# Second cross attention: the weights' products moved into the block of the turns, and another order of squares and queries

## What is computed

```
rmsnorm(x, w) = x * rsqrt(mean(x*x) + 1e-6) * w
slots = layernorm(x)                     # 16 x 64 x 256
inputs = rmsnorm(ctx, input_norm_w)      # its keys Wk and values Wv
three times:
    q     = rmsnorm(slots, slot_norm_w) @ Wq
    att   = softmax over the slots of (keys @ q * D**-0.5), normed over the keys
    u     = att summed with the values
    slots = gru_cell(u, slots, wih, whh, bih, bhh)
x = x + slots
```

## Time and profile before

| | us |
|---|---|
| three runs: median | 3616.66 |
| three runs: lowest and highest | 3610.97, 3619.45 |
| profiled execution, own time | 3608.83 |
| its span, first to last instruction | 3607.0 |
| from the start of the s1_pre block to its end, about | 1289.5 to 1299.3 |
| block of the turns, about | 1299.3 to 1798.2 |

### The profile page before, as it was taken

How to read it: one execution, slowest core, us unless ns; L and a number is a source line. 1 busy time by engine, 2 the same in 40 slices (tenths; PEclk the granted TensorE clock), 3 DMA queues, 4 the chain that set the end, 5 groups by cost and what they waited for, 6 DMA issues and landing times. The chain is left out here.

```text
span 3607.0 us, 91217 instructions
## 1 busy us (share of the span) xinstructions
PE 3381.5 (94%) x39608; PEld 2382.1 (66%) x39608; DVE 2091.1 (58%) x4136; ACT 1719.2 (48%) x3158; POOL 817.4 (23%) x464
## 2 busy tenths in 40 slices
PE   7999999979998979999989998999999789999996
PEld 4777777656676658888854455777777565665554
DVE  5666666754444257777654484556656456555337
ACT  4777777623332168887645452444444342112124
POOL 2776777410110000000031121011010003331002
PEclk9999999999999999999998999999999889999998
DMA  2111111030101415354010002112110002320530
GB/s 78 45 39 39 39 50 46 6 99 29 38 1 50 161 48 177 111 174 166 2 42 24 0 0 70 41 41 60 41 59 23 25 15 93 109 99 12 178 126 17
DMA packets 154953, 223.35 MB, mean 62 GB/s; under 512 B 39327, under 2 KB 134235, under 8 KB 154428
## 3 DMA queue, kind: packets, MB, share of 16 engines
q1 hardware_dynamic: 154556, 217.51, 18.2%
HBM read 216.44 MB, written 1.05 MB: 60 GB/s over the span
## 5 line engine op out<-in xcount | busy, mean ns | idle before, releaser
L3361 POOL TENSOR_TENSOR x_sc<-x_sc,h_T 128x2048 f32<-128x2048 f32 (+1 forms) x105 | 443.6, 4269 | 199.1 <-ACT h_T L3588 199.1
L3171 ACT ACTIVATE x_sc<-x_sc,x_nb 128x2048 f32<-128x2048 f32 (+1 forms) x112 | 210.6, 1880 | 297.5 <-DVE x_sc L3220 297.3
L3220 DVE SCALAR_TENSOR_TENSOR x_sc<-ps,x_nb,x_cap 128x2048 f32<-128x2048 f32 (+1 forms) x112 | 246.2, 2198 | 49.1 <-PE ps L3112 49.1
L3663 DVE TENSOR_TENSOR x_most<-x_most,ps 128x512 f32<-128x512 f32 (+1 forms) x352 | 234.9, 685 | 46.5 <-PE ps L3478 34.1
L1795 ACT ACTIVATE s1i_both<-ps,s_less,s_rs_s 128x64 f32<-128x64 f32 x624 | 215.0, 427 | 48.6 <-DVE s_less L1912 48.6
L3567 ACT COPY x_sc<-ps 128x1024 f32<-128x1024 f32 x192 | 179.4, 945 | 111.4 <-PE ps L3478 71.3
L3581 ACT ACTIVATE x_sc<-x_sc 128x2048 f32<-128x2048 f32 (+1 forms) x112 | 200.8, 1797 | 3.7 <-DVE x_sc L3361 3.7
L3434 PE MATMUL ps<-x_wv,x_ctx_T 128*128 128x256 f32 (+1 forms) x832 | 201.4, 383 | 0.0
L3083 PE MATMUL ps<-x_ctx_T,x_wk 128*128 128x401 f32 (+1 forms) x512 | 200.0, 517 | 1.5 <-PEq L44 1.5
L3426 PE MATMUL ps<-x_ctx_T,x_wk 128*128 128x401 f32 (+1 forms) x512 | 196.6, 522 | 4.5 <-POOL x_v L3390 3.8
L3091 PE MATMUL ps<-x_wv,x_ctx_T 128*128 128x256 f32 (+1 forms) x832 | 197.7, 379 | 0.0
(11 more groups left out here) (563 smaller groups left out, 7051.8 us busy)
## 6 DMA issues: line engine op xcount, KB each, us to landing
x_ctx_T<-in_ctx_T SPq DMA_DIRECT2D x32, 1601.0 KB
s1i_ctx_T<-in_ctx_T SPq DMA_DIRECT2D x16, 1601.0 KB, 7.1
x3i_ctx_T<-in_ctx_T SPq DMA_DIRECT2D x16, 1601.0 KB, 7.4
s1i_ctx_n<-in_ctx SPq DMA_DIRECT2D x16, 1536.0 KB
x3i_ctx_n<-in_ctx SPq DMA_DIRECT2D x16, 768.0 KB
h<-in_ctx SPq DMA_DIRECT2D x12, 896.0 KB
e_w<-in_L_attn_W SPq DMA_DIRECT2D x8, 1024.0 KB, 7.5
rows<-in_ctx SPq DMA_DIRECT2D x12, 640.0 KB
```

Source lines behind the costliest of these rows:

```text
L3171: nc.scalar.activation(x, x, ACT.Square, scale=DH ** -0.5, bias=nb[0:keys, 0:1]).then_inc(squared, 1)
L3220: nc.vector.scalar_tensor_tensor(out=slot[0:keys].rearrange("p r m h j q -> p (r m h) (j q)")[:, :, 0:width], in0=score_banks[0:keys].rear ...
L3361: return eng.tensor_tensor(x, x, most_of, ALU.subtract)
L3663: ins = nc.vector.tensor_tensor(best[0:keys, rs], best[0:keys, rs], score_banks[0:keys, rs, :, j, :], ALU.max)
```

## The change

- The block `s1_pre` and its signals go. Its work moves into the block of the turns, ahead of turn 0; only the clearing of `ssq` and the same products, roots and squares are done, none more and none less.
- PE: product for `carry`, `sum_squares(0)`, product for `wup` part 0 (banks 2 and 3), wait for `carry_out`, `carry_slots(0)`, wait for `std_ready`, product for `wup` part 1 (banks 6 and 7), wait for `combined` (part 0 taken out), `scores(0)`. Columns are now 384 and 384 where they were 512 and 256.
- ACT: the first 4 squares of pair 0 come first, then `take_carry` twice, the root for turn 0, and the rest of the squares with `take_up(0)` and `take_up(1)` between them.
- DVE: the slots' squares, 6 squares of the context, then `carry` with the input norm, the biases, `finish_prepare(0)`, 6 further squares, and 3 of pair 1.
- Turn 0: the queries of turn 1 (`prepare(1)`, `finish_prepare(1)`) come after 4 of ACT's 14 squares of pair 1 and after 6 of DVE's 12; before they came after all of them. `finish_sum(0)` moves from the start of turn 1 to between DVE's squares. `finish_sum` of the later turns stays.

```diff
-            with signals(nc, "s1_pre", "own product combined ssq_cleared") as (
-                    own, product, combined, ssq_cleared):
-                with nc.Block() as block:
...
-                        prepare(0)
+                        pe.wait_ge(weights_in, 16 * len(weights))
+                        combine_scores()
+                        sum_squares(0)
+                        combine_values(0)
+                        pe.wait_ge(carry_out, 1)
+                        carry_slots(0)
+                        pe.wait_ge(std_ready, 1)
+                        combine_values(1)
+                        pe.wait_ge(combined, KT + 1)
                         for h in range(TURNS):
                             scores(h)
...
+                        first_jobs, later_jobs = rows_job(0), rows_job(1)
                         table(env.ones[:, 0:1], ACT.Sqrt)
+                        act.wait_ge(ssq_cleared, 1)
+                        act.wait_ge(weights_in, 16 * len(weights))
+                        square(first_jobs[0])
+                        for m in range(KT):
+                            take_carry(m)
                         prepare(0)
-                        for j in rows_job(0):
-                            square(j)
+                        square(first_jobs[1])
+                        take_up(0)
+                        square(first_jobs[2])
+                        take_up(1)
+                        square(first_jobs[3])
                         norms(0)
...
                             if h == 0:
-                                for j in rows_job(1):
-                                    square(j)
+                                square(later_jobs[0])
                             if h + 1 < TURNS:
                                 prepare(h + 1)
+                                if h == 0:
+                                    for j in later_jobs[1:]:
+                                        square(j)
                                 norms(h + 1)
...
                         prepare(0)
+                        dve.wait_ge(ssq_cleared, 1)
+                        for j in first_jobs[0:2]:
+                            square(j)
+                        dve.wait_ge(weights_in, 16 * len(weights))
+                        dve.wait_ge(combined, KT)
+                        nc.vector.tensor_tensor(
+                            carry[:, :, :], carry[:, :, :],
+                            given.in_norm[:, :].unsqueeze(1).broadcast_to([P, KT, D]), ALU.mult
+                            ).then_inc(carry_out, 1)
...
                         finish_prepare(0)
-                        for j in rows_job(0):
+                        for j in first_jobs[2:4]:
                             square(j)
+                        square(later_jobs[0])
                         finish_norms(0)
                         for h in range(TURNS):
-                            if h:
+                            if h > 1:
                                 finish_sum(h - 1)
...
                             if h == 0:
-                                for j in rows_job(1):
-                                    square(j)
+                                square(later_jobs[1])
+                                finish_prepare(1)
+                                square(later_jobs[2])
+                                finish_sum(0)
+                                square(later_jobs[3])
```

More of the change, by code:

```diff
@@ L1502, in l1_xattn @@
             layernorm(nc, env, "s1_ln", env.x, env.h, env.h_T)
-            with signals(nc, "s1_pre", "own product combined ssq_cleared") as (
-                    own, product, combined, ssq_cleared):
-                with nc.Block() as block:
[L1507 to L1547, removed]
-                        steps.done(nc.vector.tensor_tensor(gb2[:, :], gb[:, 0, 0:4], gb[:, 1, 0:4],
-                                                           ALU.add))
-                        steps.wait()
-                        steps.done(nc.vector.tensor_scalar(gb2[:, :], gb2[:, :], 0.5, None,
-                                                           ALU.mult))
-                        dve.wait_ge(combined, KT)
-                        steps.done(nc.vector.tensor_tensor(
-                            carry[:, :, :], carry[:, :, :],
-                            given.in_norm[:, :].unsqueeze(1).broadcast_to([P, KT, D]), ALU.mult))
@@ L1560, in l1_xattn @@
                         "u_done u_ready u_turned u_out r_done n_done z_done gates_r n_in "
-                        "n_out gates_z updated")
+                        "n_out gates_z updated product combined carry_out ssq_cleared")
             with signals(nc, "s1", l1_turns) as (
@@ L1643, in _ @@
                                     given.load_rows(sp, pair + LANES, b)
+                    @block.gpsimd
+                    def _(pool):
+                        nc.gpsimd.memset(ssq[:, :, CT - 1], 0.0).then_inc(ssq_cleared, 1)
                     @block.tensor
@@ L1819, in other_gates, with take_carry, take_up @@
                                                      ).then_inc(gates_z, 1)
-                        table(env.ones[:, 0:1], ACT.Sqrt)
-                        prepare(0)
-                        for j in rows_job(0):
-                            square(j)
+                        def take_carry(m):
+                            act.wait_ge(product, 1)
+                            nc.scalar.activation(carry[:, m, :], ps[:, m, 0:D], ACT.Identity,
+                                                 scale=norm[:, 0, m:m + 1], bias=env.zero[:, 0:1]
+                                                 ).then_inc(combined, 1)
+                        def take_up(m):
+                            act.wait_ge(product, m + 2)
+                            bank = WUP_BANKS[m]
+                            nc.scalar.activation(
+                                wup[:, m, :].rearrange("p (c n) -> p c n", c=2),
+                                ps[:, bank:bank + 2, 0:NH3], ACT.Identity,
+                                scale=norm[:, 1, m:m + 1], bias=env.zero[:, 0:1]
+                                ).then_inc(combined, 1)
+                        first_jobs, later_jobs = rows_job(0), rows_job(1)
+                        table(env.ones[:, 0:1], ACT.Sqrt)
+                        act.wait_ge(ssq_cleared, 1)
+                        act.wait_ge(weights_in, 16 * len(weights))
+                        square(first_jobs[0])
+                        for m in range(KT):
+                            take_carry(m)
+                        prepare(0)
+                        square(first_jobs[1])
[3 more added lines that the diff above has]
+                        square(first_jobs[3])
                         norms(0)
```

37 lines of the change are left out of this document (34 added, 3 removed).

## The result

| | before | after |
|---|---|---|
| first comparison, median us | 3616.25 (6 executions) | 3597.50 (6) |
| ratio after to before, 95% interval | | 0.9953 (0.9938 to 0.9967) |
| second comparison, ratio | | 0.9966 (0.9951 to 0.9982) |
| all executions of this study: mean | 3613.6 (102) | 3599.5 (15) |
| span of the profiled execution, us | 3607.0 | 3595.6 |

The change makes the kernel faster, by 14.1 us between the means (95%: 2.2 to each side). 10.8 us were forecast; the median of 3597.5 lies 8.4 us under the forecast of 3605.9 and 2 us under the range. The executions of this study ran on several chips (0, 4, 5 and 12 are on record); each ratio compares executions of one round.

What follows compares the result with a forecast made beforehand. The prediction took the opening to be a chain of waits and steady turns to be bound by PE. Gains of 7.95 us (opening) and 2.85 us (turns 0 and 1) made 10.8: 3616.66 - 10.8 = 3605.9 us, range 3599.5 to 3612.5.

Steps and rivals of the forecast that it cites:

- Bound and chain of the opening: Opening is a chain of waits; with them filled ACT alone is late, first shift of turn 0 comes 7.9 us earlier.
- the join named: Opening, `take_up(1)`: PE's `wup` part 1 is ready at 8.8 us, just when ACT asks; each us late costs ACT one.
- the exit's 0.70 us: Between `s1_pre` and the turns: the block's own exit, 0.70 us, counted within the opening's 7.9 us gain.
- The ends of the range for `take_up`: Opening: reading two banks of 384 columns taken at the same 0.94 us; the two could cost 0 to 1.2 us more.
- a PE stall beside the transfers: Opening: SP's earlier loads run beside the products and might stall PE by 0 to 1.3 us; taken as 0.
- Turns 0 and 1: From turn 0's first shift (s), the sum of squares for turn 2 moves from s + 40.7 to 37.85: 2.85 us gained.
- Rival A: Turn 1: PE loses its clock behind a 2.2 us pause, turn 2's scores start slowly, 1.5 to 2.4 us lost; chance 0.15.
- The sum for the stage: Opening plus turns 0 and 1: 7.95 + 2.85 = 10.8 us gained, with nothing found that takes it back.
- from this sum on all runs at the old distances: After turn 2's sum of squares: later turns unchanged and bound by PE, so the 10.8 us gain stays.
- B: Opening: joins cost 2.5 us through late `wup` part 1 or dearer `take_up`; gain 6.5 to 8.5 us; chance 0.13.
- C: Pair changes: halves come late behind new loads, turns lengthen by 2.27 us; up to 2.8 us slower overall; chance 0.04.
- D: Opening: programs overlap less than drawn, as moved rows aren't ready or waits keep the old order; gain 0 to 5; chance 0.08.

Runs made afterwards that it cites:

- `m_order`: Changed kernel with the old order inside its one block (products, all taken out, root, then squares); second cross attention 6.9 us longer than the changed kernel's mean.
- `v_counts`: Changed kernel with halves' squares taken 1, 1, 2, 2, 1, 1 to a turn instead of 2, 1, 1, 2, 1, 1; median 3598.0 us beside the changed kernel's 3597.5.
- `b_warm`: Kernel before with PE's holes in the opening filled by matmuls whose result nobody reads; median 3611.8 against 3612.1 us, ratio 0.9998.
- `e_turn`: Kernel before with only the edits of turns 0 and 1, `s1_pre` block kept; second cross attention 2.9 us shorter than before.
- `e_open`: Changed kernel with turns 0 and 1 as before, so the new opening alone; second cross attention 501.0 us against 509.5 before.

## Why the prediction was right or wrong

- **Bound and chain of the opening: right.** Removing waits, no work, gave 8.5 us against 7.9. ACT was the bound, PE late for it by 0.46 us at the join named; the prediction had called a wait there a sign of being wrong, and it was one by 0.46 us only. Under-sized was the merging itself, put down at the exit's 0.70 us only; in the old order it is 1.8 us (`m_order`). The ends of the range for `take_up` (0 to 1.2 us more) and for a PE stall beside the transfers (0 to 1.3) were not needed: 0.99 us each, and none.
- **Turns 0 and 1: right in what is late next, 0.4 us too large.** 2.45 us (40.7 to 38.25) against 2.85. Root for turn 1 at s + 14.4 (13.9 said), scores at 16.9 (16.3), E1 at 25.6 (25.2). The half us comes from the slow weighted sum ahead of it (36 records in 6.46 us, 5.62 before): PE summed the slots' squares at s + 13.6, where the prediction had them done by then. That ACT's squares are late next is shown by `v_counts`. The prediction put the gain down to the scores no longer starting late; `b_warm` leaves that start where it was and has S2 at 38.22. So what the hole cost was PE's slow clock behind it, and starting the scores earlier is one way of two to be rid of that.
- **Rival A: happened, and cost nothing here.** The clock fell in turn 1, but at the weighted sum, behind a pause of 2.03 us:

```profile
1334.00:1336.00 2.00, 0.05 (x1) 1.00 0.36 122
1336.00:1338.00 2.00, 1.92 (x12) 0.65 0.03 8
1338.00:1340.00 2.00, 2.00 (x13) 0.50 0.00 0
```

  36 records took 5.82 us, and PE still waited 0.50 us for DVE behind them. The prediction let the 2.11 us row speak against a fall; it doesn't, as a single row of a pause without one says nothing of the next. The Trainium skill (TensorE: Matmul & The Clock Gate, "HAM oscillation — how this bites in real kernels") describes a kernel whose bursts each start slow again behind the pause for a transfer; the changed kernel has one in turn 1, at 0.50 behind 2.03 us, and the earlier trace rows has a pause behind which there is none. It cost nothing, since the burst had 2 us in hand. In `e_turn` the fall came where rival A had put it, at the queries of turn 2, and cost 1.4 us of that turn (21.0 for 19.6 us), near the 1.5 to 2.4 said.
- **The sum for the stage: right.** 10.8 us against 11.2. That the parts measured alone give 11.4 is no proof of it: they overlap by 1.7 us at S2, and single profiles of one kernel differ by 1.1 to 2.2 us.
- **The step that failed: "from this sum on all runs at the old distances", carried to the end of the program.** It holds to the end of the changed stage (10.9 us at S2, 11.2 at the end). Beyond it the lengths of four stages spread by 3.3 to 7.7 us each over the 20 profiles. The 8.4 us between forecast and median come apart so: 3.1 from the median of three runs that the gain was taken off (3616.7, where 102 executions have a mean of 3613.6), 2.0 from the six executions after (3597.5 against a mean of 3599.5 in all 15), 0.4 from the changed stage, and 2.9 from the others. The first two are spread of the measurement, which the range was to hold. The 2.9 us are the step that failed, and their size is known to 2.2 us either way; why these stages move stays open. With it fell the assumption that one profiled execution stands for the medians: both early profiles of the kernel before (3607.0, 3607.2) were the shortest of a spread of 3607 to 3620 in five. That PE's clock had low stretches in these stages (0.81 to 0.99 on average in each) stood in the profile and went unread. The range took 3 to 4 us of measurement to each side, which is about the standard deviation of a single execution (4.1 us), and nothing for stages that move.
- **Rivals B, C and D** didn't come: 0.46 us at the join instead of 2.5; the turn at the first pair change took 21.1 us where it took 21.9. That such a turn can get longer when the turns shift, as rival C had it, is seen elsewhere: 23.2 us in `e_open`, and the 21.3 us of `b_warm`.

## What to carry to other kernels

In an opening that is a chain of waits, lay the engines' programs side by side and count the busiest engine's work: with the waits filled, the time is that work plus the joins, and each join's lateness is read directly. After a change, compare stage by stage first: a stage that isn't touched can move by several us, and by more than the error of the sum. Take several profiles of the kernel before, not one, ahead of any forecast of its median. And read a run that fills a hole at the place where it acts: the median of `b_warm` says that the clock costs nothing, its rows say 2.4 us in turns 0 and 1, most of it lost again in turn 17.

## What was not expected of the hardware

One unchanged program, or one that shifts by 1 to 11 us early on, has another granted clock of PE in stages 1000 to 2000 us later: the last stage has 0.86, 0.81 or 0.75 of full clock and takes 94.5, 99.5 or 102.2 us. Raising the mean granted clock by 0.0027 with idle matmuls bought no time at the median (3611.8 against 3612.1), though 2.4 us in the turns where they stood. And the clock fell to the lower level, 1.2 GHz, behind a pause of 2.03 us, where it stayed at the upper one behind 2.11 us.
